# A graph attention layer on one core: the exponent's table, the running bound D and the small exponentials handled in another order

## The reference

```python
h = jnp.maximum(_layernorm(x, axis=-1), 0.0)
# inside the graph layer
h = h @ W.T
src = h @ a1
dst = h @ a2
e = jax.nn.leaky_relu(src[:, None] + dst[None, :], negative_slope=0.2)
e = jnp.where(adj == 0, jnp.float32(-9e15), e)
attention = jax.nn.softmax(e, axis=1)
return x + attention @ h
```

## Time and profile before

| | |
|---|---|
| profiled execution's own time | 384.0 us |
| span of its core | 382.4 us |
| median of the runs | 383.94 us |
| PE busy | 376.6 us, 98% |
| DVE busy | 362.8 us, 95% |
| ACT busy | 195.7 us, 51% |
| granted clock of PE | full in all 40 slices |
| chain that ended last, by engine | PE 96%, ACT 1%, DMA 1%, issue 1% |
| stretch 34 to 40 us | PE 5.57, DVE 5.48, ACT 5.53 us busy of 6.00 |
| stretch 40 to 41.5 us | PE 0.64, DVE 1.50, ACT 1.50 us busy of 1.50 |
| stretch 41.5 to 50 us | PE 8.39, DVE 8.50, ACT 5.39 us busy of 8.50 |

### The profile page before, as it was taken

The page is one execution under the profiler, slowest core; times in us unless marked ns, Lnnn a source line. Parts: engine busy times, 40 slices in busy tenths (PEclk is TensorE's granted clock), DMA queues, the critical chain, the costliest instruction groups (busy, mean ns, idle before and its releaser), DMA issues.

```text
span 382.4 us, 9231 instructions
## 1 busy us (share of the span) xinstructions
PE 376.6 (98%) x3358; PEld 330.5 (86%) x3358; DVE 362.8 (95%) x456; ACT 195.7 (51%) x272; POOL 43.1 (11%) x68
## 2 busy tenths in 40 slices
PE   8999899999999999999999999999999999999996
PEld 6788688888888888888888888888888888888885
DVE  4999999999999999999999999999987999999965
ACT  5999754744443644344445543444446443444430
POOL 3897020000000001110000002100000011100001
PEclk9999999999999999999999999999999999999999
DMA  7931476857676666776666667766665567666503
GB/s 252 374 78 42 136 228 223 278 165 233 221 222 215 210 218 221 235 231 224 220 218 205 216 209 234 239 222 222 216 208 184 169 216 244 232 219 225 171 2 111
DMA packets 27025, 78.23 MB, mean 205 GB/s; under 512 B 3956, under 2 KB 9336, under 8 KB 27000
## 3 DMA queue, kind: packets, MB, share of 16 engines
q1 hardware_dynamic: 25568, 74.59, 60.4%
q0 software_dynamic: 1280, 3.16, 2.2%
q10 hardware_dynamic: 152, 0.13, 0.1%
HBM read 73.66 MB, written 4.21 MB: 204 GB/s over the span
## 4 chain that ended last, share of the span: by engine, by line
PE 96%; ACT 1%; DMA 1%; issue 1%; DVE 0%; ACTq 0%
PE ps L1435 88%; PE ps L1259 2%; PE ps L1274 2%; PE ps L1285 2%; PE ps L1280 2%; DMA a_rows<-a 1%; PE ps L1224 1%; PE ps L1240 1%; ACT c_row L517 0%; ACT h_sb L491 0%; DVE rows_sb L1153 0%; ACT L643 0%; ACT p_hi L527 0%; ACTq L502 0%; PE ps L1234 0%
## 5 line engine op out<-in xcount | busy, mean ns | idle before, releaser
L1435 PE MATMUL ps<-v_sb,p_hi 128*128 (+2 forms) x2048 | 251.9, 273 | 1.0 <-ACT p_hi L527 0.9
L537 ACT ACTIVATE p_hi<-p_sb,gp 128x1024 f16<-128x1024 f32 x126 | 144.4, 1149 | 166.5 <-DVE p_sb L816 140.0
L1435 PEld LDWEIGHTS ps<-v_sb,p_hi 128*128 128x128 f16 x2048 | 199.6, 98 | 26.9 <-issue 1.2
L823 DVE SCALAR_TENSOR_TENSOR p_lo<-p_sb,gp,p_hi 128x1024 f16<-128x1024 f32 x126 | 160.7, 1277 | 7.2 <-ACT p_hi L537 6.7
L816 DVE SCALAR_TENSOR_TENSOR p_sb<-c_row,gp,adj_sb 128x1024 f32<-128x1024 uint32 (+1 forms) x126 | 160.5, 1278 | 0.0
L1435 PE MATMUL ps<-v_sb,p_lo 128*128 (+1 forms) x1024 | 141.6, 273 | 0.0
L1435 PEld LDWEIGHTS ps<-v_sb,p_lo 128*128 128x128 f16 x1024 | 100.0, 98 | 12.8 <-DVE p_lo L823 0.2
L467 POOL DMA_DIRECT2D out<-rows_sb x24 | 13.0, 541 | 263.0 <-DVE rows_sb L1117 262.9
L416 POOL TENSOR_SCALAR hn_sb<-x_sb,moments,rstd 128x256 f32<-128x256 f32 x17 | 21.3, 1260 | 4.1 <-DVE rstd L765 3.2
L775 DVE SCALAR_TENSOR_TENSOR hnt_lo<-ps,hnt_hi 128x256 f16<-128x256 f32 x32 | 12.9, 410 | 0.3 <-ACT hnt_hi L507 0.2
L1274 PE MATMUL ps<-w_hi,hnt_hi 128*128 128x258 f16 x64 | 12.5, 277 | 0.4 <-ACT h_sb L491 0.4
(11 more groups left out here) (87 smaller groups left out, 87.9 us busy)
## 6 DMA issues: line engine op xcount, KB each, us to landing
adj_sb<-adj_t SPq DMA_DIRECT2D x128, 512.0 KB, 4.8
x_sb<-x SPq DMA_DIRECT2D x7, 512.0 KB, 8.5
out<-rows_sb POOLq DMA_DIRECT2D x24, 128.0 KB, 4.6
c_row<-c_flat SPq DMA_DIRECT2D x3, 512.0 KB, 6.7
out<-rows_sb SPq DMA_DIRECT2D x7, 128.0 KB, 1.8
x_sb<-x SPq DMA_DIRECT2D x2, 256.0 KB, 3.5
c_row<-s_flat SPq DMA_DIRECT2D x1, 512.0 KB, 3.9
w_nat<-w SPq DMA_DIRECT2D x1, 256.0 KB, 2.8
```

The lines of the kernel that those rows point to most:

```text
L537: nc.scalar.activation(p_hi[:, u % R, :], p_sb[:, u % R, :], ACT.Copy, scale=p_scale[:, bass.ds(t, 1)])\
L823: nc.vector.scalar_tensor_tensor(out=p_lo[:, u % R, :], in0=p_sb[:, u % R, :], scalar=p_scale[:, bass.ds(t, 1)], in1=p_hi[:, u % R, :], op ...
L1435: return nc.tensor.matmul(ps[:, k, 0:width], part[:, u % R, k * P:(k + 1) * P], v_sb[:, bass.ds(t, 1), v, 0:width], start=start, stop=stop ...
```

## The change

`LATE` grows to 5, so D's spread scores cover tiles 27 to 31, and the scores kept in `h_sb` are needed up to tile 26 only. The spread is made in two: tiles 27 to 29 (384 columns) into `bank_d`, and tiles 30 and 31 (256 columns) into `bank_e`; `turn_d` goes to the free 128 columns of `bank_d`. `d_top` reduces those 512 columns, and `d_last`, in the place of `d_early`, the 256 of `bank_e`. The table's load moves ahead of `keep_h(27)`, straight behind `split_hn_hi(31)`. The destination exponentials are taken by ACT from `h_sb` itself, with the scale and the bias as operands held in SBUF (`exp_g` and `exp_p`, two instructions in the place of `exp_gp`, each for tiles 0 to 3 and again for 4 to 31); DVE's four `gp_args` instructions go, and one for `p_bias` comes. `exp_c` has three parts of 256, 256 and 512 columns instead of four. Tiles 30 and 31 are projected into `bank_d` and `bank_e`, once DVE has reduced these. `keep_h` stays on ACT for all tiles, as before. `value_lo(10)` moves from ahead of the first weights to behind `split_lo(6)`.

```diff
-    LATE = 4
+    LATE = 5
+    SPREAD = 3
+    EXP_PARTS = ((0, 2), (2, 4), (4, 8))
+        own_banks = {T - 2: bank_d, T - 1: bank_e}
...
+        def h_in_psum(t):
+            return ps[:, own_banks.get(t, bank_h + t % 2), 0:FW]
...
-            for n, factor in enumerate((-0.8, 0.8, -0.8 * H_DOWN)):
+            for n, factor in enumerate((-0.8, 0.8, -0.8 * H_DOWN, 0.2)):
...
-            def exp_gp(tiles, n):
-                act.wait_ge(gp_args_ready, n)
-                nc.scalar.activation(gp[:, :, tiles], gp_args[:, :, tiles], ACT.Exp).then_inc(gp_ready, 1)
+            def exp_g(t0, t1):
+                act.wait_ge(c_bias_ready, 1)
+                act.wait_ge(*kept(t1 - 1))
+                nc.scalar.activation(g_col[:, t0:t1], h_sb[:, t0:t1, F + 1], ACT.Exp,
+                                     bias=exp_bias[:, 0:1], scale=exp_scale[:, 1:2]).then_inc(g_ready, 1)
+            def exp_p(t0, t1):
+                act.wait_ge(p_bias_ready, 1)
+                act.wait_ge(*kept(t1 - 1))
+                nc.scalar.activation(p_scale[:, t0:t1], h_sb[:, t0:t1, F + 1], ACT.Exp,
+                                     bias=p_bias[:, 0:1], scale=exp_scale[:, 3:4]).then_inc(p_scale_ready, 1)
...
             split_hn_hi(31)
+            nc.scalar.activation(table_ready[:], eps_sb[:], ACT.Exp)
             keep_h(27)
-            nc.scalar.activation(table_ready[:], eps_sb[:], ACT.Exp)
...
-                    dve.wait_ge(gp_ready, 1)
+                    dve.wait_ge(g_ready, 1)
...
+            nc.vector.tensor_scalar(p_bias[:], exp_bias[:], 0.25, math.log(P_UP), ALU.mult, ALU.add).then_inc(p_bias_ready, 1)
+            split_hn_lo(31)
...
             def project_hi(t):
                 pe.wait_ge(hnt_hi_ready, t + 1)
-                if t >= 2:
+                if t in own_banks:
+                    pe.wait_ge(d_top_ready, 1)
+                    pe.wait_ge(d_last_ready, 1)
+                elif t >= 2:
                     pe.wait_ge(*kept(t - 2))
...
-                        if t == 0 and k == bank_h:
-                            pe.wait_ge(*kept(T - 2))
-                        if t == 0 and k == bank_h + 1:
-                            pe.wait_ge(*kept(T - 1))
+                        if t == 0 and k in (bank_h, bank_h + 1):
+                            pe.wait_ge(*kept(T - 4 + (k - bank_h)))
+                        if t == 0 and k in (bank_d, bank_e):
+                            pe.wait_ge(*kept(T - 2 + (k - bank_d)))
```

More of the change, by code:

```diff
@@ L142, in gat_layer @@
         d_top = sb("d_top", [P, 1])
-        d_early = sb("d_early", [P, 1])
+        d_last = sb("d_last", [P, 1])
         d_safe = sb("d_safe", [P, 1])
-        gp_args = sb("gp_args", [P, 2, T])
+        p_bias = sb("p_bias", [P, 1])
         gp = sb("gp", [P, 2, T])
@@ L239, in gat_layer @@
         s_loaded = sem("s_loaded")
[L240 removed]
+        g_ready = sem("g_ready")
+        p_scale_ready = sem("p_scale_ready")
         v_lo_ready = sem("v_lo_ready")
@@ L490, in keep_h @@
                 act.wait_ge(h_done, t + 1)
-                nc.scalar.activation(h_sb[:, t, :], ps[:, bank_h + t % 2, 0:FW], ACT.Copy, scale=H_DOWN)\
+                nc.scalar.activation(h_sb[:, t, :], h_in_psum(t), ACT.Copy, scale=H_DOWN)\
                     .then_inc(h_kept, 1)
@@ L641, in _ @@
             split_hn_hi(31)
+            nc.scalar.activation(table_ready[:], eps_sb[:], ACT.Exp)
             keep_h(27)
-            nc.scalar.activation(table_ready[:], eps_sb[:], ACT.Exp)
+            exp_g(0, R)
+            exp_c(0)
             keep_h(28)
-            exp_c(0)
+            exp_p(0, R)
+            exp_c(1)
+            hi_part(0, 0)
             keep_h(29)
-            exp_gp(slice(0, R), 1)
-            exp_c(1)
             exp_c(2)
-            hi_part(0, 0)
-            exp_c(3)
             hi_part(0, 1)
             keep_h(30)
+            keep_h(31)
             hi_part(0, 2)
-            keep_h(31)
             hi_part(0, 3)
@@ L663, in _ @@
                 .then_inc(c_col_ready, 1)
-            exp_gp(slice(R, T), 2)
-            act.wait_ge(gp_ready, 2)
+            exp_g(R, T)
+            exp_p(R, T)
+            act.wait_ge(p_scale_ready, 2)
             split_hi(3, 3, 0)
@@ L967, in _ @@
                 .then_inc(d_part_ready, 1)
+            split_hn_lo(30)
+            dve.wait_ge(d_some_spread, 1)
+            dve.wait_ge(d_turned, 1)
+            nc.vector.tensor_reduce(d_top[:], ps[:, bank_d, 0:(SPREAD + 1) * P], AX.X, ALU.max).then_inc(d_top_ready, 1)
             dve.wait_ge(d_all_spread, 1)
-            nc.vector.tensor_reduce(d_top[:], ps[:, bank_d, 0:LATE * P], AX.X, ALU.max).then_inc(d_top_ready, 1)
-            dve.wait_ge(d_turned, 1)
-            nc.vector.tensor_reduce(d_early[:], ps[:, bank_e, 0:P], AX.X, ALU.max).then_inc(d_early_ready, 1)
+            nc.vector.tensor_reduce(d_last[:], ps[:, bank_e, 0:(LATE - SPREAD) * P], AX.X, ALU.max).then_inc(d_last_ready, 1)
             dve.wait_ge(d_top_ready, 1)
-            dve.wait_ge(d_early_ready, 1)
-            nc.vector.tensor_scalar(d_safe[:], d_top[:], d_early[:, 0:1], D_MARGIN, ALU.max, ALU.add).then_inc(d_safe_ready, 1)
-            dve.wait_ge(scales_ready, 5)
+            dve.wait_ge(d_last_ready, 1)
+            nc.vector.tensor_scalar(d_safe[:], d_last[:], d_top[:, 0:1], D_MARGIN, ALU.max, ALU.add).then_inc(d_safe_ready, 1)
+            dve.wait_ge(scales_ready, 6)
             dve.wait_ge(d_safe_ready, 1)
@@ L993, in _ @@
             low_part(1, 0)
[L994 to L997, removed]
             edge_weights(2, 2, 16, 0)
@@ L1019, in _ @@
             split_lo(6, 6, 0)
+            value_lo(10)
             dve.wait_ge(p_lo_ready, 5)
@@ L1279, in project_w_lo @@
                 for c in range(KC):
-                    nc.tensor.matmul(bank_of(t), turned("hi", t)[:, c, :], w_lo[:, c, 0:FW], start=False, stop=False)
+                    nc.tensor.matmul(h_in_psum(t), turned("hi", t)[:, c, :], w_lo[:, c, 0:FW], start=False, stop=False)
             def project_lo(t):
@@ L1284, in project_lo, with spread_d @@
                 for c in range(KC):
[L1285 removed]
+                    last = nc.tensor.matmul(h_in_psum(t), turned("lo", t)[:, c, :], w_hi[:, c, 0:FW],
                                             start=False, stop=(c == KC - 1))
                 last.then_inc(h_done, 1)
[L1289 removed]
+            def spread_d(out, t0, t1, ready):
                 pe.wait_ge(w2_ready, 1)
[L1291 to L1292 removed]
+                pe.wait_ge(hnt_hi_ready, t1)
+                a = t0 % RT * P
                 for c in range(KC):
[L1294 removed]
+                    last = nc.tensor.matmul(out, w2_hi[:, c, :], hnt_hi[:, c, a:a + (t1 - t0) * P],
                                             start=(c == 0), stop=(c == KC - 1))
[L1296 removed]
+                last.then_inc(ready, 1)
             def turn_d():
                 pe.wait_ge(d_part_ready, 1)
[L1300 removed]
+                nc.tensor.transpose(ps[:, bank_d, SPREAD * P:(SPREAD + 1) * P], d_up[:, 0:1].to_broadcast([P, P]), ident[:])\
+                  .then_inc(d_turned, 1)
             keep_busy(bank_h, 3)
```

32 lines of the change are left out of this document (13 added, 19 removed).

## The result

The changed kernel took 384.87 us, the kernel before 384.14 (medians of 22 runs each); the recorded ratio is 1.0016, with a 95% interval of 1.0008 to 1.0023 (the two medians divided give 1.0019). It is slower, by 0.3 to 0.9 us. The prediction was 384.2 in a range of 383.2 to 384.8, a 0.23 us loss beside the 383.94 it started from, and put most of its weight on no change that can be told. The ratio applied to that 383.94 gives 384.55, inside the range; the 384.87 as it stands is 0.07 above the range's end. The profiled execution has a span of 383.3 us, 0.9 more than before.

A forecast was written before the change was run, and what follows sets the result against it. The prediction took DVE's queue from about 40.8 to 48.8 us to set the end. A 0.52 us delay less 0.29 won made 384.0 + 0.23 = 384.23 us own time, hence 384.2 us, range 383.2 to 384.8.

The forecast's parts named there:

- What bounds: Handover to PE's products: DVE's queue from about 40.8 to 48.8 us sets the end, not the first product's start.
- D's chain: D's scores up to the bias: d_up takes an earlier slot and exp_bias ends at 37.86 us, 0.31 earlier.
- The table: ACT's table load behind the high split: starts at 35.84 us, next copy 1.40 later, 0.38 slack, off the path.
- rival E: ACT's table load: ScalarE pays twice, by a second load or a drain; exp_g 0.89 us later, 385.1 us; chance 0.07.
- ACT's queue: ACT from bias to last c_row piece: short exponentials 0.41 us each, wide exp_c(2) 0.79, ending at 41.23.
- C: Rival on ACT: small exponentials at the old gp row's price, 0.42 us off the queue, 383.8 us; chance 0.15.
- DVE's hole: DVE before tile 0's third weight piece: it waits for exp_c(2), so low_part(0, 0) starts 0.52 us later, at 42.08.
- The sum of the handover: PE's low products of tile 2: 0.52 us later less 0.29 won from gp_args, 0.23 us later, at 49.12.
- value_lo(10): DVE behind split_lo(6): costs 0.61 us but is hidden by DVE's 1.0 us lead over PE; without cover 0.6.

The follow-up runs named there:

- e3: Changed kernel with keep_h(28) moved ahead of exp_g and keep_h(29) behind hi_part(0, 1) in ACT's order: 384.40 us, ratio 1.0012 to the kernel before.
- e11: Changed kernel with tiles 30 and 31 projected into the shared banks 6 and 7 again: 384.87 us, ratio 1.0019 to the kernel before.
- e5: Changed kernel with the table's load back behind keep_h(27): 385.72 us, ratio 1.0044 to the kernel before.
- e6: Kernel before with only the table's load moved ahead of keep_h(27): 385.10 us, ratio 1.0028 to the kernel before.
- e1: Kernel before with only value_lo(10) moved from ahead of the first weights to behind split_lo(6): 384.66 us, ratio 1.0017.
- e2: Changed kernel with value_lo(10) back ahead of the first weights: 384.04 us, ratio 1.0003 to the kernel before.
- e12: Changed kernel with value_lo(10) early, keep_h(28) and keep_h(29) moved, and value_lo(12) on GpSimd behind the stores of c: 384.24 us, ratio 1.0008 to the kernel before.
- e8: Changed kernel with value_lo(10) early, keep_h(28) and keep_h(29) moved, and value_lo(30) on GpSimd: 384.92 us, ratio 1.0027 to the kernel before.
- e9: Changed kernel with value_lo(10) early, keep_h(28) and keep_h(29) moved, and value_lo(12) on GpSimd behind value_hi(12): 383.84 us, ratio 0.9996 to the kernel before.

## Why the prediction was right, and where it was short

- *What bounds.* Right in kind, wrong in reach. The queue of DVE decides and not the first product (e3, e11). But I let it end at 48.8 us and wrote that from there PE is behind DVE's supply for good. DVE's hold lasts to the change of groups at 126 us, as each `value_lo` in between takes 0.6 us from DVE's lead, more than two tiles of 2.39 against 2.64 us give back.
- *D's chain*: bias 0.31 us earlier by forecast, 0.31 from A measured. *The table*: 1.41 us from load to copy, nothing beside it; rival E did not happen. The Trainium skill (ScalarE: Activation LUTs, What ACT_TABLE_LOAD costs) names a drain of 1.38 us with each switch. No row here shows one: in e5 the load starts 0.01 us behind the end of the copy before it. I missed that the load may stand there only because `d_up` no longer needs tile 27 (e6).
- *ACT's queue*: the short exponentials 0.39 and 0.38 for a forecast of 0.41, the wide part 0.80 for 0.79. The Trainium skill (ScalarE: Activation LUTs, What ACT_TABLE_LOAD costs) adds 93 ns for each operand in SBUF, which makes an estimate of 0.375 us; the rows' 0.39 and 0.38 agree. C did not happen.
- *DVE's hole*: `low_part(0, 0)` 0.52 later by forecast, 0.47 from A. *The sum of the handover*: 0.23 by forecast, 0.18 measured.
- *`value_lo(10)`*: this step failed. The prediction said that "by then DVE has gained 4 x 0.25 = 1.0 us on PE, so it is hidden; without that cover it would cost 0.6". It cost 0.58 (e1) and 0.61 (e2). The cover was read at the place where the instruction stands, not at the place where the lead is smallest. Behind `split_lo(6)` DVE is 0.95 us ahead of PE (its low split ends at 58.49, PE takes it at 59.44), but at tile 16 only 0.35, of which 0.06 remain even where PE waits, and at the change of groups PE already loses 0.18 us in the kernel before. The term mis-sized is this one, 0 for 0.6; with it the loss would have been 0.23 + 0.6, that is 384.8.
- *What was luck*: that the time can be read as inside the range. The range's upper end was built from unknown costs that came out as forecast (the short exponentials, the wide one, `d_last`); nothing in it stood for `value_lo(10)`, which used up that room.

## What to carry to other kernels

When work is moved into the queue of an engine that keeps another one fed, look for the smallest lead on the whole way behind it, up to the next point at which both meet, and not for the lead where it is put; an instruction that left an idle moment was free only there. Before a handover is judged by the first instruction of the bound engine, follow the supplier's queue: here 0.9 us at the first product cost nothing, and 0.5 us at the last columns of `c_row`, for which DVE's fourth weight piece waits, cost 0.5. And an edit to one engine's order is checked against every wait for what it delays, not against its own queue alone.

## What the runs showed of the hardware

GpSimd's `tensor_tensor` with two inputs in SBUF and DVE's `scalar_tensor_tensor` did not run side by side: in e12 DVE's instruction grew by 1.24 us beside one of 1.14, in e8 POOL's stretched to 7.56. The Trainium skill (SBUF — State Buffer, Who interferes with whom) says that only the port pair which DVE and GpSimd share causes contention, as an exclusive lock; the rows agree that one waits for the other, and which port it is they can't show. What I had not expected is who wins. In e8 POOL's instruction stood through five of DVE's that followed each other without a gap, 1.29 us each as ahead of it. It ended at 121.81; if it then took the 1.14 us of e12 (an estimate), it ran from 120.67, about where DVE waited for ACT between its last pair of low splits, and that pair took 0.77 us longer. In e12 and e9 DVE was the one that grew, and in e12 its row begins 0.30 us ahead of POOL's, so the order of the rows' starts does not tell who waits. What lets POOL in between two of DVE's instructions, the runs don't show.
